# Row sums of a graph layer turned by VectorE and DMA instead of TensorE, with two large loads issued from ScalarE's queue

## The reference

```
h   = relu(layernorm(x))                                    # 512 x 128
HW  = h @ W[r, :128] + sum_d(W_edges[r, d] * W[r, 128 + d]) # r = 0..6; the second term is a row c_r
A   = [adj, adj, shifted, adj^T, adj^T, shifted^T, eye]
out = x + max over r of (A[r] @ HW[r]) + b
```

## Time and profile before

| | us |
|---|---|
| median of 3 runs | 211.2 (208.2 to 211.62) |
| the profiled execution | 208.36 |
| its span, first to last instruction | 206.6 |
| PE busy | 198.2 (96%) |
| DVE busy | 178.8 (87%) |
| ACT busy | 162.3 (79%) |
| POOL busy | 130.0 (63%) |
| granted TensorE clock | 1.00 of full |

### The profile page before, as it was taken

How to read it: one execution, slowest core, us unless ns; L and a number is a source line. 1 busy time by engine, 2 the same in 40 slices (tenths; PEclk the granted TensorE clock), 3 DMA queues, 4 the chain that set the end, 5 groups by cost and what they waited for, 6 DMA issues and landing times.

```text
span 206.6 us, 3426 instructions
## 1 busy us (share of the span) xinstructions
PE 198.2 (96%) x922; PEld 152.2 (74%) x922; DVE 178.8 (87%) x411; ACT 162.3 (79%) x432; POOL 130.0 (63%) x166
## 2 busy tenths in 40 slices
PE   6999999799999999999999999999999999999991
PEld 6556468568788787878878787877878786887871
DVE  3587869999889998999889998999989999997565
ACT  3987989597979969696997969698896969685230
POOL 4140246969593977939594696919695486959600
PEclk9999999999999999999999999999999999999999
DMA  6999999987896959699795969779695969923201
GB/s 183 311 360 361 361 359 270 304 268 224 312 293 187 387 127 392 153 336 263 244 351 140 389 126 368 218 257 342 210 352 100 396 136 295 261 91 47 65 2 51
DMA packets 33747, 51.07 MB, mean 247 GB/s; under 512 B 1872, under 2 KB 11328, under 8 KB 33728
## 3 DMA queue, kind: packets, MB, share of 16 engines
q1 hardware_dynamic: 31152, 46.53, 66.2%
q0 software_dynamic: 2304, 4.20, 13.1%
q10 hardware_dynamic: 272, 0.13, 0.2%
HBM read 46.65 MB, written 4.19 MB: 246 GB/s over the span
## 4 chain that ended last, share of the span: by engine, by line
PE 70%; DMA 11%; DVE 6%; SPq 4%; POOL 3%; issue 3%; ACT 0%; DVEq 0%; ACTq 0%; POOLq 0%
PE bank_p L846 10%; PE bank_p L847 8%; PE bank_p L848 8%; DMA x_bias<-in_biasT_dram 8%; PE bank_g L809 5%; PE bank_g L811 5%; PE bank_g L817 5%; PE bank_gT L800 5%; PE bank_gT L794 5%; PE bank_gT L791 5%; DMA x_bias<-in_xT_dram 4%; PE bank_p L836 3%; PE bank_p L733 3%; PE bank_p L741 2%; DVE best L632 2%
## 5 line engine op out<-in xcount | busy, mean ns | idle before, releaser
L330 POOL TENSOR_TENSOR a_lo<-adj_sb,a_hi 128x512 fp32r<-128x512 f32 x28 | 36.1, 1310 | 38.0 <-DVE h_lo L601 36.9
L337 POOL TENSOR_TENSOR aT_lo<-adjT_sb,aT_hi 128x512 fp32r<-128x512 f32 x28 | 39.5, 1575 | 0.0
L632 DVE TENSOR_TENSOR best<-bank_p,best 128x512 f32<-128x512 f32 x48 | 33.2, 691 | 5.8 <-PE bank_p L848 4.7
L414 ACT ACTIVATE a_hi<-adj_sb 128x512 fp32r<-128x512 f32 x56 | 34.5, 620 | 0.0
L423 ACT ACTIVATE aT_hi<-adjT_sb 128x512 fp32r<-128x512 f32 x56 | 34.4, 620 | 0.0
L629 DVE SCALAR_TENSOR_TENSOR best<-bank_p,c_col,best 128x512 f32<-128x512 f32 x32 | 23.9, 748 | 5.0 <-ACT best L472 4.4
L595 DVE TENSOR_TENSOR aT_lo<-adjT_sb,aT_hi 128x512 fp32r<-128x512 f32 x28 | 25.4, 945 | 0.0
L435 ACT ACTIVATE h<-x_sb,shift,rstd 128x128 f32<-128x128 f32 x60 | 24.6, 488 | 0.0
L323 POOL TENSOR_TENSOR o_sb<-best,x_bias 128x512 f32<-128x512 f32 x15 | 20.8, 1384 | 3.4 <-DMA x_bias<-in_xT_dram 3.4
L846 PE MATMUL bank_p<-hT_hi,w_hi 128*128 128x512 f32 x48 | 20.1, 420 | 0.4 <-ACT sumsT L465 0.4
L588 DVE TENSOR_TENSOR a_lo<-adj_sb,a_hi 128x512 fp32r<-128x512 f32 x28 | 20.3, 765 | 0.0
(11 more groups left out here) (118 smaller groups left out, 493.9 us busy)
## 6 DMA issues: line engine op xcount, KB each, us to landing
adj_sb<-in_adj_dram SPq DMA_DIRECT2D x15, 1024.0 KB, 5.5
adjT_sb<-in_adjT_dram SPq DMA_DIRECT2D x15, 1024.0 KB, 7.1
x_bias<-in_biasT_dram SPq DMA_DIRECT2D x16, 256.0 KB, 4.8
x_bias<-in_xT_dram POOLq DMA_DIRECT2D x16, 256.0 KB, 5.1
x_sb<-in_x_dram SPq DMA_DIRECT2D x15, 256.0 KB, 7.9
out_dram<-o_sb SPq DMA_DIRECT2D x15, 256.0 KB, 4.1
adj_sb<-in_adj_dram SPq DMA_DIRECT2D x4, 256.0 KB, 4.4
adjT_sb<-in_adjT_dram SPq DMA_DIRECT2D x4, 256.0 KB, 4.8
```

The lines of the kernel that those rows point to most:

```text
L330: nc.gpsimd.tensor_tensor(a_lo[q][:, c, :], adj_sb[q][:, c, :], a_hi[q][:, c, :].bitcast(F32), ALU.subtract).then_inc(alo_last_ready, 1)
L337: nc.gpsimd.tensor_tensor(aT_lo[q][:, c, :], adjT_sb[q][:, c, :], aT_hi[q][:, c, :].bitcast(F32), ALU.subtract).then_inc(aTlo_last_ready, 1)
L414: nc.scalar.activation(a_hi[q][:, c, :], adj_sb[q][:, c, :], ACT.Copy, accum_out=sums[q][:, 0, c:c + 1]).then_inc(ahi_ready, 1)
L632: op = nc.vector.tensor_tensor(best[q][:, :], product, best[q][:, :], ALU.max)
```

## The change

For b >= 2 (`TURNED = 2`) the row sums no longer go through POOL, PE, PSUM and ACT:

- DVE, in `turn_blocks(b+1)` between its third and fourth maximum of graph b, copies the sums rounded (16 numbers in a partition), subtracts them for the lo part, and transposes the 128x32 tile in 32x32 blocks.
- SP, in `turn_sums(b)`, writes these 16 KB to a scratch tensor in DRAM, waits for its landing, and reads them back with four small DMAs (each four rows of 512 numbers, in pieces of 32 numbers) into `sumsT`, of which there are now two. PE waits for them in `begin_products`.
- PE drops L741, ACT drops `copy_sumsT`, POOL drops `part_sums` for these graphs.
- POOL waits for `aTlo_ready` of graph b, DVE's part of `aT_lo`, ahead of `finish(b-1)`.
- `adj` and `adjT` of graph b+2, for b >= 1, are issued from ACT's queue: `load_adj` after `std_of`, ahead of `make_h`; `load_adjT` after `begin_best`. `std_of(b+2)` moves behind `split_gT` and `split_hT`.
- In graph 1, DVE takes all six maxima first, then `split_adj_lo(2)`, `scale_and_shift(3)` and `turn_blocks(2)`.

```diff
@@ SP @@
+            def turn_sums(b):
+                i = b - TURNED + 1
+                q = b % 2
+                sp.wait_ge(blocks_turned, i)
+                sp.dma_start(scratch, sum_blocks[:, :]).then_inc(scratch_in, 16)
+                sp.wait_ge(scratch_in, 16 * i)
+                sp.wait_ge(prod_psum, (b - 1) * NPROD)
+                for g in range(len(ORDER_A)):
+                    sp.dma_start(sumsT[q][g * GROUP:g * GROUP + 4, :].rearrange("r (c j s) -> r c j s", c=C, s=GROUP)
+                                 .bitcast(F32), scratch_rows[g // 2]).then_inc(sumsT_in[q], 16)
             for b in range(1, B):
+                if b >= TURNED:
+                    turn_sums(b)
                 if b + 3 < B:
                     load_x(b + 3)
-                if b + 2 < B:
-                    load_adj(b + 2)
                 store(b - 1)
                 if b + 1 < B:
                     load_bias(b + 1)
-                if b + 2 < B:
-                    load_adjT(b + 2)
@@ POOL @@
             for b in range(1, B):
                 if b >= 2:
+                    pool.wait_ge(aTlo_ready, (b - FIRST + 1) * ND)
                     finish(b - 1)
...
-                    part_sums(b + 1)
@@ ACT @@
                 if 2 <= b < B - 1:
                     split_adj(b + 1)
+                split_gT(b)
+                split_hT(b)
                 if 2 <= b < B - 2:
                     std_of(b + 2)
-                split_gT(b)
-                split_hT(b)
+                if b + 2 < B:
+                    load_adj(b + 2)
                 if b + 1 < B:
                     make_h(b + 1)
                 split_g(b)
-                copy_sumsT(b)
+                if b < TURNED:
+                    copy_sumsT(b)
                 begin_best(b)
+                if b + 2 < B:
+                    load_adjT(b + 2)
@@ DVE @@
+            def turn_blocks(b):
+                q = b % 2
+                i = b - TURNED + 1
+                s = sums[q][:, :, :].unsqueeze(2).to_broadcast([P, 2, 2, C])
+                dve.wait_ge(ahi_ready, (b - FIRST + 1) * NS)
+                dve.wait_ge(aThi_ready, (b - FIRST + 1) * NS)
+                nc.vector.tensor_copy(sum_cols[:, :, :, 0, :], s).then_inc(cols_hi, 1)
+                dve.wait_ge(cols_hi, i)
+                nc.vector.tensor_tensor(sum_cols[:, :, :, 1, :], s, sum_cols[:, :, :, 0, :].bitcast(F32),
+                                        ALU.subtract).then_inc(cols_lo, 1)
+                dve.wait_ge(cols_lo, i)
+                if i >= 2:
+                    dve.wait_ge(scratch_in, 16 * (i - 1))
+                nc.vector.transpose(sum_blocks[:, :], sum_cols[:, :, :, :, :].rearrange("p d k s c -> p (d k s c)")
+                                    .bitcast(F32)).then_inc(blocks_turned, 1)
...
-            take_best(1, 1)
-            take_best(1, 2)
+            for i in range(1, NPROD):
+                take_best(1, i)
             split_adj_lo(2)
             scale_and_shift(3)
-            for i in range(NH, NPROD):
-                take_best(1, i)
+            turn_blocks(2)
...
                 for i in range(1, NPROD - int(b == B - 1)):
+                    if i == NH + 1 and b + 1 < B:
+                        turn_blocks(b + 1)
                     take_best(b, i)
@@ PE @@
             def begin_products(b):
-                pe.wait_ge(sumsT_ready, b + 1)
+                if b < TURNED:
+                    pe.wait_ge(sumsT_ready, b + 1)
+                else:
+                    pe.wait_ge(sumsT_in[b % 2], 64 * (b // 2))
...
-                turn_sums(b)
+                if b < TURNED:
+                    turn_sums(b)
```

More of the change, by code:

```diff
@@ L83, in gnn_kernel @@
         sum_parts = pair("sum_parts", [P, C, 2, 2, GROUP], F32R)
-        sumsT = sb("sumsT", [P, N], F32R)
+        sumsT = pair("sumsT", [P, N], F32R)
+        sum_cols = sb("sum_cols", [P, 2, 2, 2, C], F32R)
+        sum_blocks = sb("sum_blocks", [P, GROUP])
         x_bias = pair("x_bias", [P, N])
@@ L179, in gnn_kernel @@
         sumsT_ready = sem("sumsT_ready")
+        cols_hi = sem("cols_hi")
+        cols_lo = sem("cols_lo")
+        blocks_turned = sem("blocks_turned")
+        scratch_in = sem("scratch_in")
+        sumsT_in = [sem(f"sumsT_in{i}") for i in range(2)]
         hT_psum = sem("hT_psum")
@@ L264, in _ @@
             sp.dma_start(w_sb[:, 5:7, :], w_dram[:, 0:2, :]).then_inc(wa_in, 16)
-            load_adj(1)
-            load_adjT(1)
+            sp.dma_start(adj_sb[1][:, :, :], adj_dram[1]).then_inc(adj_in[1], 16)
+            sp.dma_start(adjT_sb[1][:, :, :], adjT_dram[1]).then_inc(adjT_in[1], 16)
             load_x(2)
@@ L411, in split_adj @@
                     act.wait_ge(gT_psum, b - 1)
-                act.wait_ge(parts_lo, b - 1)
+                if b < 2 + TURNED:
+                    act.wait_ge(parts_lo, b - 1)
+                else:
+                    act.wait_ge(cols_lo, b - 1 - TURNED)
                 for c in range(C):
@@ L462, in copy_sumsT @@
                 act.wait_ge(sumsT_psum, b + 1)
-                if b >= 1:
-                    act.wait_ge(prod_psum, b * NPROD)
-                nc.scalar.activation(sumsT[:, :], bank_s[:, 0:N], ACT.Copy).then_inc(sumsT_ready, 1)
+                nc.scalar.activation(sumsT[b % 2][:, :], bank_s[:, 0:N], ACT.Copy).then_inc(sumsT_ready, 1)
             def begin_best(b):
@@ L473, in begin_best, with load_adj, load_adjT @@
                                      bias=c_col[:, ORDER[0]:ORDER[0] + 1]).then_inc(best_begun, 1)
+            def load_adj(b):
+                q = b % 2
+                if b - 2 < FIRST:
+                    act.wait_ge(sums_ready, 2 * (b - 2) + 1)
+                act.wait_ge(gT_psum, b - 1)
+                if b >= 2 + FIRST:
+                    act.wait_ge(alo_ready, (b - 1 - FIRST) * ND)
+                    act.wait_ge(alo_last_ready, (b - 1 - FIRST) * NG)
+                act.dma_start(adj_sb[q][:, :, :], adj_dram[b]).then_inc(adj_in[q], 16)
+            def load_adjT(b):
+                q = b % 2
+                if b - 2 < FIRST:
+                    act.wait_ge(sums_ready, 2 * (b - 2) + 2)
+                act.wait_ge(g_psum, b - 1)
+                if b >= 2 + FIRST:
+                    act.wait_ge(aTlo_ready, (b - 1 - FIRST) * ND)
+                    act.wait_ge(aTlo_last_ready, (b - 1 - FIRST) * NG)
+                act.dma_start(adjT_sb[q][:, :, :], adjT_dram[b]).then_inc(adjT_in[q], 16)
             act.dma_start(x_sb[0][:, HALF:, :], x_dram[0][:, HALF:, :]).then_inc(x0_in[1], 16)
@@ L826, in begin_products @@
                 for i in range(NH, NPROD - int(b == B - 1)):
-                    add_sums(i, bank_of[i], start=True)
+                    add_sums(b, i, bank_of[i], start=True)
                 if b == B - 1:
@@ L830, in begin_products, with add_sums @@
                     for nodes, to in zip(HALVES, last_banks):
-                        add_sums(NPROD - 1, to, nodes, start=True)
-            def add_sums(i, to, nodes=slice(0, N), start=False, stop=False):
+                        add_sums(b, NPROD - 1, to, nodes, start=True)
+            def add_sums(b, i, to, nodes=slice(0, N), start=False, stop=False):
                 group = ORDER_A.index(ORDER[i])
                 rows = slice(group * GROUP, (group + 1) * GROUP)
-                return nc.tensor.matmul(to[:, nodes], c_rows[rows, :], sumsT[rows, nodes], start=start, stop=stop)
+                return nc.tensor.matmul(to[:, nodes], c_rows[rows, :], sumsT[b % 2][rows, nodes], start=start, stop=stop)
             def passes(i, dst, nodes=slice(0, N), start=False, stop=False):
@@ L856, in product @@
                     pe.wait_ge(wlo_ready, 1)
-                if i == 2:
+                if i == 2 and b < TURNED:
                     pe.wait_ge(sumsT_ready, b + 1)
```

44 lines of the change are left out of this document (14 added, 30 removed).

## The result

The changed kernel takes 231.76 us in the median of four runs (227.25 to 234.56), the one before 211.41 (208.2 to 211.99): 1.0955 times the time of before, 95% interval 1.0836 to 1.1074. The forecast was 204.5, range 200.5 to 213.5. Two of the four runs, the profiled one of 234.56 among them, fell in a slower state of the program, so the ratio rests on the other two, 227.25 and 230.12.

The account below looks back on a forecast made before the run. PE was taken to bound the kernel, DVE nearest. From 208.36, eleven rounds save 4.2, the last two 0.9, the third graph 0.2: 203.1, plus half the 2.8 run-level gap, 204.5 us; range 200.5 to 213.5.

Parts of the forecast that it names:

- The engines' terms: Steady round by engine: PE 11.35, DVE's loop 11.36 with turn_blocks at 0.5, plus ACT's issue cost; 11.50 taken.
- PE's round without L741: Dropping the four matmuls L741 saves PE 0.45 a round, from 11.80 to 11.35.
- ACT's issues: DMA issues on ACT ahead of make_h might delay its activations, bounds 0 to 0.47 for an issue.
- the 0.16 at L836: PE waits at L836 for DVE's late g_lo, losing 0.16, which makes a round of 11.50.
- the DVE wait of 0.3: DVE waits 0.3 for aT_hi before turn_blocks, which makes a DVE round of 11.65.
- the sums' way through DRAM: Scratch write and reads: 2.72 + 1.4 + two landings of 3.0 give a loop of 10.1, hidden; shows from 3.6 each.
- The late-sums rival: Sums reach PE too late: landings of 4.1 make a round of 12.3 and a time of 212.1; chance 0.10.
- 8.1: Estimate for the sums' DRAM loop with a fixed 2.0 us per DMA: 2.7 + 1.4 + 4.0, never seen.
- The rival of the meeting: turn_blocks' subtraction waits some 1.3 behind POOL's aT_lo: a DVE loop of 12.66, 215.9 us; chance 0.15.
- The loads' move: adj and adjT issued from ACT: store and bias on SP start some 0.5 later, covered by POOL's idle time.
- The third graph: At the start, maxima first on DVE remove PE's 1.45 wait for bank_g: gain 0.2, bounds 0 to 1.9.
- other engines take the gain: DVE and ACT, level with PE, keep the round at 11.88: 207.3, or 208.7 with 1.4 on top; chance 0.28.

Follow-up runs that it names:

- e14: Changed kernel with POOL's aT_lo waiting for turn_blocks, bias added after it, and adj and adjT loads from graph 3 on cut to a quarter: 0.9663, 201.4 us.
- e7: Changed kernel with no work for the sums from graph 2 on (no turn_blocks, no scratch DMAs), loads on ACT: 206.53 us, 0.9856.
- e9: Changed kernel with scratch in rows (2 KB reads), POOL's aT_lo waiting for turn_blocks and bias added after it: 217.59 us, 1.0412.
- e10: Changed kernel, scratch still in 128-byte pieces, with POOL's aT_lo waiting for turn_blocks and bias added after it: 233.68 us, 1.1027.
- e17: Changed kernel, POOL's order kept, with adj and adjT loads from graph 3 on cut to a quarter of their bytes: 1.1069.
- e4: Kernel before, with adj and adjT loads issued from ACT's queue and std_of moved; sums as before: 212.44 us, 1.0184.
- e12: Kernel before, with the new DVE order in graph 1 (all six maxima first): 209.82 us, 1.004.
- e5: Changed kernel without scratch DMAs, turn_blocks kept but unused, and POOL waiting for turn_blocks before adding the bias: 208.72 us, 0.9989.
- e8: Kernel before, with the work for the sums left out from graph 2 on, loads on SP: 208.02 us, 0.9947.
- e2: Changed kernel without any scratch DMAs for the sums, turn_blocks kept with its result unused: 235.42 us, 1.1317.

## Why the prediction was wrong

**The engines' terms were right.** PE's round without L741 was forecast at 11.35; it is 11.33 in e14, e7 and the rounds of e9 with punctual sums. turn_blocks was 0.5 and is 0.54 to 0.55. ACT's issues (0.37 each) cost nothing, the lower bound of 0 to 0.47, so that the 0.16 at L836 and the DVE wait of 0.3 don't exist. From ACT's operation ahead of each issue to the one behind it are 0.48 and 0.59, where they were 0.48 and 0.58 without an issue. For that case the prediction had "the rounds are 11.35 and the time nearer 201.5", and e14 took 201.4. These terms only show when both of the following are gone.

**The step that failed: the sums' way through DRAM.** It took 3.0 per landing, "hidden", with 10.1 for the loop. The form of the loop was right (2.72 + issues + two landings); three values in it were not. Until the fourth read is issued it takes 2.62 - 0.61 = 2.0 in place of 1.4: that was read from loads of 256 KB, and a read in 64 pieces takes 0.61 to issue. The landings, counted from there as in the forecast, were 3.57 and 4.58 + 0.61 = 5.2 in the round shown, 5.5 and 6.7 in the long one of e10. And "the reads fall where the `adjT` load is over" left out `adj`: it is issued at 94.95, while the four reads are being issued, and needs 5.8 us (median), to about when they land; `adjT`, issued at 98.32 and 7.7 us on its way, lies over the next write at 104.44. The nearest row was the one I set aside, 0.4 KB in 3.5 us among other loads; 3.0 was under it. The DMA share of 0.85 to 0.87 left some 1.7 us of a round quiet (an estimate), while the write's landing and the four issues need 1.4 + 2.6 even with light loads. The late-sums rival had the right mechanism, at 212.1 and a chance of 0.10; with these values its own sum, 2.72 + 2.0 + 3.57 + 5.2 = 13.5, gives the measured round.

The Trainium skill (DMA: Bandwidth & Descriptors, Issuing engines are not separate DMA queues) says that DMAs started by different engines run on the same 16 engines and interleave. The trace agrees: SP's write of 16 KB landed in 1.4 each time beside light loads from ACT's queue (e14) and in up to 5.7 beside full ones (e10). The same page of the Trainium skill (Latency and other measured facts) has 0.2 us for an access to HBM and 2 at high load; no run here splits a landing, but 1.4 with light loads against a median of 2.3 and up to 4.8 with full ones goes the same way. The fixed 2.0 of the same page of the Trainium skill (Anatomy of one DMA), from which I had worked out 8.1, is given there for DMAs issued by GpSimd. Beside full loads both of SP's landings in the round shown were longer, and the loop took 13.5.

**The rival of the meeting was underpriced.** It was a wait of "some 1.3" and a chance of 0.15, from one piece of POOL, and only for the subtraction, which reads two tiles. Measured are 3.1 to 3.3, mostly in the copy, which reads one: it waits through POOL's DMA issue and both pieces. In e17 that gives rounds of 14.16, and 1.107. That POOL comes before DVE was seen as the exception; with the bias on time POOL issues at 110.81 and DVE copies at 111.11, and so in ten of e17's fourteen rounds. The Trainium skill (SBUF — State Buffer, SBUF: two separate sides) has the lock held for one whole instruction. Here the two pieces and the issue pass as one, so a price from one instruction is too low.

**Why two causes of 10% or more make 10%.** Late sums hold DVE and SP back, SP's bias comes later, and POOL then runs after turn_blocks: in the round shown it waits 4.48 for the bias and issues at 105.64, where turn_blocks began at 103.79. The meeting is rare (5 rounds). Punctual sums bring it back (e17). So taking away either one uncovers the other. The order of these steps is read from the traces; no run moved the bias alone in the changed kernel.

**The loads' move was costed at a small delay of store and bias that "POOL idles ahead of `a_lo`" would cover.** It isn't covered: in the changed kernel the bias is issued behind the write's landing and the issue of the four reads, beside the megabytes of ACT's queue, its median landing goes from 4.8 to 5.7, and POOL waits 37.0 us for it (9.2 before). By e4 the loads' move alone is 1.8% (0.8 to 2.9).

**The third graph** was a gain of 0.2 (0 to 1.9). It hangs on POOL's order. Graph 2's round took 14.79 before, and 0.45 less without L741 would be 14.34. It takes 14.2 in e9 and e14, where POOL's bias comes last and the sums are on time: a gain of 0.1. In POOL's old order it takes 15.43 in e12, where the bias is late and DVE's `aT_lo` lasts 3.89 beside POOL's, and 16.18 in the changed kernel (at a granted clock of 0.89), where two waits for POOL stand:

```profile
41.64 0.49 PE L858 MATMUL bank_g<-aT_lo,h_hi 128*128 128x512 f32 x1 [1.70 <-POOL aT_lo L334]
42.86 0.79 PE L858 MATMUL bank_g<-aT_lo,h_hi 128*128 128x512 f32 x1 [0.72 <-POOL aT_lo L334]
```

**The rival "other engines take the gain"** was right for the kernel without the two causes but with the old order of POOL: e5 at 0.999 and e8 at 0.995, rounds of 11.7, where DVE's `aT_lo` meets POOL's (1.75 in e5). By itself it would have eaten the 5.3 us of the forecast.

What stays open: how a late landing divides between the DMA engines' queues and the memory, why PE's waits for the sums rose from 15.1 to 28.3 us with POOL's other order (e10), and whether the full loads can be timed so that the write and the reads find a quiet moment.

## What to carry to other kernels

A transfer that something waits for is priced by what else the DMA engines carry at that moment, not by its bytes: 16 KB took 1.4 us in a quiet queue and up to 5.7 beside two loads of 1 MB, and a round trip through DRAM pays this twice in series, plus the issue of each piece. A small VectorE operation that reads SBUF must be ordered against GpSimd's run of work, not only its next instruction. And where one cause is removed and nothing moves, remove the next one too before it is called innocent: a two-by-two of experiments showed here what single ones hid.

## What the hardware showed beyond that

- A DVE copy of 128x16 took 3.1 to 3.3 us (e2, e17) when it began during a POOL DMA issue that two POOL operations followed, and 0.16 without them.
- Issuing a read of 8 KB in 64 pieces takes SP 0.61 us, in four rows of 2 KB 0.30; a 1 MB load takes ACT 0.37, and ACT's next activation started no later (steps of 0.48 and 0.59, before 0.48 and 0.58).
- After 5.5 us without a matmul (69.32 to 74.83 in e10) the granted clock was 0.50 from 74 to 78, so that a late DMA costs PE more than its wait.
